# Scan products in 64x32 tiles over two banks each, one bank for gate/up and one for projections, and a new order of work in a tick

## The reference, cut to what matters

```python
# B=2, S=4096, D=512, H=16 heads of Dh=32; mini-batches of MB=16 tokens
k = rope(x @ Wk.T);  v = x @ Wv.T             # per head
W = eye(Dh)                                   # one state per batch and head
for kc, vc in minibatches(k, v):              # 256 steps, one after the other
    z = kc @ W
    W = W - kc.T @ ((z - vc) * (2.0 / (MB * Dh)))
out = (layernorm(zs) * ln_gamma + ln_beta) @ Wo.T
x1 = layernorm(x + out)
h = silu((x1 @ gate_w.T) * gate_s) * ((x1 @ up_w.T) * up_s)      # 1408 wide
y = layernorm(x1 + (h @ down_w.T) * down_s)
```

## Time and profile before

| | |
|---|---|
| median of 3 runs | 2142.03 us (2141.74 to 2142.14) |
| span of the profiled execution | 2140.6 us |
| instructions | 46538 |
| PE busy / PE weight loads busy | 2034.7 us / 1564.8 us |
| DVE / ACT / POOL busy | 1197.3 / 895.1 / 602.6 us |
| mean DMA rate | 82 GB/s |

### The profile page before, as it was taken

The page is one execution under the profiler, slowest core; times in us unless marked ns, Lnnn a source line. Parts: engine busy times, 40 slices in busy tenths (PEclk is TensorE's granted clock), DMA queues, the critical chain, the costliest instruction groups (busy, mean ns, idle before and its releaser), DMA issues.

```text
span 2140.6 us, 46538 instructions
## 1 busy us (share of the span) xinstructions
PE 2034.7 (95%) x16272; PEld 1564.8 (73%) x16272; DVE 1197.3 (56%) x2814; ACT 895.1 (42%) x2258; POOL 602.6 (28%) x651
## 2 busy tenths in 40 slices
PE   7569999999999999999999999999999999999998
PEld 4347777777777777777777777777777777777677
DVE  3575556555556555555655555655555655555553
ACT  2334444444434444434444434444434444444432
POOL 2002323232323232323222323222333322233223
PEclk9779999999999999999999999999999999999999
DMA  7742232212322212232212232212232212232210
GB/s 229 237 133 59 90 87 80 75 52 72 87 89 80 75 52 70 86 89 80 86 39 72 85 91 80 85 48 63 85 90 82 84 50 72 74 90 74 56 35 21
DMA packets 210943, 175.78 MB, mean 82 GB/s; under 512 B 34192, under 2 KB 165520, under 8 KB 210576
## 3 DMA queue, kind: packets, MB, share of 16 engines
q1 hardware_dynamic: 210768, 173.08, 27.0%
HBM read 105.86 MB, written 75.76 MB: 85 GB/s over the span
## 4 chain that ended last, share of the span: by engine, by line
PE 88%; DVE 4%; issue 3%; SPq 3%; ACT 2%; DMA 1%; DVEq 0%; POOL 0%; POOLq 0%; ACTq 0%
PE gu_acc L563 34%; PE work L547 25%; PE down_acc L572 13%; PE z_acc L526 7%; PE state_acc L539 7%; PE work L554 3%; DVE err L722 2%; SPq L290 2%; ACT state L420 2%; DMA z_scr<-v_rows 1%; DVE low_half L733 1%; SPq L275 0%; DMA x_tok<-wkT 0%; DMA z_tok<-z_scr 0%; DMA k_scr<-k_tok 0%
## 5 line engine op out<-in xcount | busy, mean ns | idle before, releaser
L722 DVE TENSOR_TENSOR err<-z_acc,v_rows 32x256 f32<-32x256 f32 x1024 | 430.6, 421 | 736.4 <-PE z_acc L526 700.0
L382 POOL TENSOR_TENSOR hid_lo<-hid,hid_hi 128x256 fp32r<-128x256 f32 x352 | 285.1, 810 | 769.0 <-ACT hid_hi L456 769.0
L420 ACT ACTIVATE state<-state_acc 32x256 f32<-32x256 f32 x1028 | 386.7, 376 | 251.8 <-PE state_acc L539 222.8
L438 ACT ACTIVATE v_rows<-z_acc 128x256 f32<-128x256 f32 x256 | 98.7, 385 | 716.0 <-DVE err L722 716.0
L563 PE MATMUL gu_acc<-x_hi,gw 128*128 128x256 f32 x1408 | 381.8, 305 | 0.5 <-DVE x_lo L780 0.5
L563 PE MATMUL gu_acc<-x_lo,gw 128*128 128x256 f32 x1408 | 346.2, 280 | 0.0
L563 PE MATMUL gu_acc<-x_hi,uw 128*128 128x256 f32 x1408 | 346.0, 279 | 0.0
L563 PE MATMUL gu_acc<-x_lo,uw 128*128 128x256 f32 x1408 | 345.8, 279 | 0.0
L563 PEld LDWEIGHTS gu_acc<-x_hi,gw 128*128 128x128 f32 x1408 | 264.9, 188 | 100.0 <-issue 98.1
L572 PE MATMUL down_acc<-dw,hid_hi 128*128 128x512 f32 x704 | 287.5, 408 | 0.0
L572 PE MATMUL down_acc<-dw,hid_lo 128*128 128x512 f32 x704 | 278.6, 396 | 0.0
(11 more groups left out here) (67 smaller groups left out, 2170.8 us busy)
## 6 DMA issues: line engine op xcount, KB each, us to landing
x_fm<-xT SPq DMA_DIRECT2D x64, 256.0 KB, 4.2
k_scr<-k_tok SPq DMA_DIRECT2D x32, 512.0 KB, 5.1
k_rows<-k_scr SPq DMA_DIRECT2D x512, 32.0 KB, 2.2
v_rows<-v_scr SPq DMA_DIRECT2D x512, 32.0 KB, 1.8
z_scr<-v_rows SPq DMA_DIRECT2D x512, 32.0 KB, 1.6
z_tok<-z_scr SPq DMA_DIRECT2D x32, 512.0 KB, 4.1
x_tok<-x SPq DMA_DIRECT2D x32, 512.0 KB, 3.8
out<-x_tok SPq DMA_DIRECT2D x32, 512.0 KB, 2.8
```

Source lines behind the costliest of these rows:

```text
L382: pool.tensor_tensor(hid_lo[m % RING][:], hid[m % 2][:], hid_hi[m % RING][:].bitcast(F32), ALU.subtract).then_inc(hid_lo_ready, 1)
L420: act.activation(state[q, :, q], state_acc[q, 0:NG * HEAD].rearrange("p (g e) -> p g e", g=NG), ACT.Copy, scale=-STEP).then_inc(state_read ...
L438: act.activation(v_rows[:, i].rearrange("p g c -> p (g c)"), z_acc[:, 0:2 * P], ACT.Copy).then_inc(z_saved, 1)
L722: dve.tensor_tensor(err[q, 2 * j:2 * j + 2, :, :].rearrange("p g h e -> p (g h e)"), z_acc[q, 0:2 * P], v_rows[q, i].rearrange("p g c -> p ...
```

## The change

1. **Scan products.** A 128-row product becomes two 64-row ones in the upper and the lower half of the array (`tile_position=(r*64, j*32)`), so eight tiles of 64x32 work side by side. The block of `state` that a 64-row half needs is 64 wide in place of 128, and the part of `err` that it needs is 128 wide in place of 256. The halves r=0 and r=1 write to two different banks, so `z_acc` and `state_acc` take two banks each. `scan_z` goes from 8 products of 128 columns to 16 of 64, `scan_state` from 4 of 256 to 8 of 128. DVE and ACT read both banks in the same number of instructions, of the same 256 elements for each partition.
2. **Banks.** To free two banks, gate/up has one (`gu_acc`) and the projection scratch has one (`work`). Piece m+1 of gate/up waits until DVE has read piece m (`hid_ready`), and each of batch 1's projections and turns waits until batch 0's result has been read. The turns of x1 go to `gu_acc`.
3. **Order.** Gate/up is in slots 0 to 8, 11 and 13, `down` in 1 to 9, 13 and slot 0 of the next tick; v of batch 1 is projected in quarters in slots 1 to 4, the k turns are in slots 5 and 6, the z turns in 7 and 8, wo in 9 and 10, wk of batch 0 in 12, v of batch 0 in 14 (so a tick earlier than before), wk of batch 1 in 15, the x1 turns in 14 and 15. The scaling of y, its residual and its norm move to slots 1 to 4 of the next tick. DVE, ACT, POOL and the DMA queue follow that order.
4. On PE the values of the scan's waits are computed ahead of the waits (`ahead`).

```diff
--- before.py
+++ after.py
+GU_SLOTS = (0, 1, 2, 3, 4, 5, 6, 7, 8, 11, 13)
+DOWN_SLOTS = (1, 2, 3, 4, 5, 6, 7, 8, 9, 13)
...
-        err = sb("err", [P, NG, HQ, HEAD])
-        state = sb("state", [P, NG, P])
+        err = sb("err", [P, NG // 2, HQ, HEAD])
+        state = sb("state", [P, NG, 2 * HEAD])
...
-        state_acc = bank("state_acc")
-        z_acc = bank("z_acc")
-        gu_acc = [bank("gu_acc0"), bank("gu_acc1")]
+        def bank_pair(name):
+            return ctx.enter_context(nc.psum_tensor(name, [P, 2, 512], F32))
+
+        state_acc = bank_pair("state_acc")
+        z_acc = bank_pair("z_acc")
+        gu_acc = bank("gu_acc")
         down_acc = [bank("down_acc0"), bank("down_acc1")]
-        work = [bank("work0"), bank("work1")]
...
                 if ncc.within():
-                    store_z(ncc, 1, saved[1], z_sent[1])
+                    store_z(ncc, 1, saved[1])
+                if t.within():
+                    if t.past(2):
+                        for half in range(2):
+                            sp.wait_ge(rows_in[half], rows_b)
+                    sp.wait_ge(v_ready, v_first)
+                    sp.dma_start(v_scr[t.par, 0], v_tok[0][:]).then_inc(v_stored, 16)
+                if ncc.within():
+                    sp.wait_ge(z_stored, z_sent[1])
                     if ncc.past(1):
                         sp.wait_ge(zn_turned, c_before)
                     sp.dma_start(z_tok[:], z_scr[:, rows(ncc), :].rearrange("b t f -> t b f")).then_inc(z_tok_in, 16)
+                if t.within():
+                    sp.wait_ge(k_ready, split)
+                    sp.dma_start(k_scr[t.par].rearrange("b t f -> t b f"), k_tok[:]).then_inc(k_stored, 16)
                 if nb.within():
                     if nb.past(1):
                         sp.wait_ge(state_added, scanned)
                     load_rows(nb.par, 1, k_sent[1], v_sent[1])
+                if t.back(-1).within() and t.past(0):
+                    load_x_fm(t.back(-1), split, used)
...
+                if t.within():
+                    sp.wait_ge(v_ready, split)
+                    sp.dma_start(v_scr[t.par, 1], v_tok[1][:]).then_inc(v_stored, 16)
...
+                    if ncc.within() and s == 11:
+                        inverse_root(1, ncc)
+                    if nd.within() and s - 1 in GU_SLOTS:
+                        low_hid(nd, GU_SLOTS.index(s - 1))
+                    if t.within() and s == 1:
+                        add_rotated(t, 1)
+                    if ny.within() and s in (1, 2):
+                        add_residual(ny, s - 1)
+                    if ny.within() and s == 3:
+                        inverse_root(2, ny)
...
+                    if ncc.within() and s in (7, 8):
+                        add_bias(ncc, s - 7)
+                    if nk.within() and s == 13:
+                        add_rotated(nk, 0)
...
-                    act.activation(state[q, :, q], state_acc[q, 0:NG * HEAD].rearrange("p (g e) -> p g e", g=NG),
+                    e = slice(h % 2 * HEAD, (h % 2 + 1) * HEAD)
+                    act.activation(state[q, :, e].rearrange("p (r g) e -> p r g e", r=2),
+                                   state_acc[q, :, 0:P].rearrange("p r (g e) -> p r g e", e=HEAD),
                                    ACT.Copy, scale=-STEP).then_inc(state_ready, 1)
...
+                    if nd.within() and s - 1 in GU_SLOTS:
+                        high_hid(nd, GU_SLOTS.index(s - 1))
+                    if nk.within() and s == 10:
+                        high_x(nk, ncc, 0)
+                    if ncc.within() and s == 8:
+                        high_zn(ncc, t, 1)
+                    if nb.within():
+                        if s % 2 == 0:
+                            save_z(nb, s // 2)
+                        else:
+                            act.wait_ge(state_added, nb.count(4 * NS, 4 * (s // 2) + 4))
+                            copy_state()
+                    if nd.within() and s in GU_SLOTS:
+                        gate(nd, GU_SLOTS.index(s))
+                    if t.within() and s == 4:
+                        copy_v(t, 1)
+                    if ncc.within() and s == 7:
+                        high_zn(ncc, t, 0)
+                    if nk.within() and s == 10:
+                        high_x(nk, ncc, 1)
+                    if nk.within() and s == 14:
+                        copy_v(nk, 0)
+                    if ncc.within() and s in (14, 15):
+                        high_x1(ncc, s - 14)
...
             def scan_z(n, i):
+                loaded, saved, turned = [ahead(v) for v in (n.count(4 * NS, 4 * i + 4), n.count(NS, i), n.count(4, 4))]
+                pe.wait_ge(zeroed, 6)
                 if i == 0:
-                    pe.wait_ge(k_cols_ready, n.count(4, 4))
-                pe.wait_ge(state_ready, n.count(4 * NS, 4 * i + 4))
+                    pe.wait_ge(k_cols_ready, turned)
+                pe.wait_ge(state_ready, loaded)
                 if i >= 1 or n.past(1):
-                    pe.wait_ge(z_saved, n.count(NS, i))
-
-                for g in (*range(0, NG, 2), *range(1, NG, 2)):
-                    j = g // 2
-                    mm = pe.matmul(z_acc[j * HEAD:(j + 1) * HEAD, g % 2 * P:(g % 2 + 1) * P],
-                                   lhsT=k_cols[n.par][:, g, i, :], rhs=state[:, g, :], start=True, stop=True,
-                                   skip_group_check=True, tile_position=(0, j * HEAD))
-                    if g % 2:
-                        mm.then_inc(z_done, 1)
+                    pe.wait_ge(z_saved, saved)
+
+                for odd in range(2):
+                    for r in range(2):
+                        k = slice(r * P // 2, (r + 1) * P // 2)
+                        for j in range(NG // 2):
+                            g = 2 * j + odd
+                            mm = pe.matmul(z_acc[j * HEAD:(j + 1) * HEAD, r, odd * 2 * HEAD:(odd + 1) * 2 * HEAD],
+                                           lhsT=k_cols[n.par][k, g, i, :], rhs=state[k, g, :], start=True, stop=True,
+                                           skip_group_check=True, tile_position=(r * P // 2, j * HEAD))
+                            if odd and r:
+                                mm.then_inc(z_done, 1)
             def scan_state(n, i):
+                loaded, ready = ahead(n.count(32 * NG, 32 * NG)), ahead(n.count(4 * NS, 4 * i + 4))
+                pe.wait_ge(zeroed, 6)
                 if i % (NS // 2) == 0:
-                    pe.wait_ge(rows_in[i // (NS // 2)], n.count(32 * NG, 32 * NG))
-                pe.wait_ge(err_ready, n.count(4 * NS, 4 * i + 4))
-                for h in range(HQ):
-                    q = slice(h * HEAD, (h + 1) * HEAD)
-                    pe.matmul(state_acc[q, 0:NG * HEAD], lhsT=k_rows[:, i, q], rhs=err[:, :, h, :],
-                              start=False, stop=False, skip_group_check=True, tile_position=(0, h * HEAD)
-                              ).then_inc(state_added, 1)
+                    pe.wait_ge(rows_in[i // (NS // 2)], loaded)
+                pe.wait_ge(err_ready, ready)
+                for r in range(2):
+                    k = slice(r * P // 2, (r + 1) * P // 2)
+                    for h in range(HQ):
+                        q = slice(h * HEAD, (h + 1) * HEAD)
+                        mm = pe.matmul(state_acc[q, r, 0:P], lhsT=k_rows[k, i, q], rhs=err[k, :, h, :],
+                                       start=False, stop=False, skip_group_check=True,
+                                       tile_position=(r * P // 2, h * HEAD))
+                        if r:
+                            mm.then_inc(state_added, 1)
...
+            def gate_up(n, m, dt):
+                if m == 0:
+                    pe.wait_ge(x1_lo_ready, n.count(2, 2))
+                else:
+                    pe.wait_ge(hid_ready, n.count(NM, m))
...
+            def turn_z(n, t, b):
+                pe.wait_ge(zn_ready, n.count(2, b + 1))
+                if b == 1:
+                    pe.wait_ge(zn_low, n.count(2, 1))
+                elif t.within():
+                    pe.wait_ge(k_cols_ready, t.count(4, 4))
+                else:
+                    pe.wait_ge(o_added, n.count(2))
+                turn(work, z_tok, b, zn_turned)
+            def project_o(n, b):
+                if b == 0:
+                    if not n.past(1):
+                        pe.wait_ge(w_low, 3 * NC)
+                    pe.wait_ge(zn_low, n.count(2, 2))
+                else:
+                    pe.wait_ge(o_added, n.count(2, 1))
+                project(b, wo, o_done)
+            def turn_x1(n, nd, b):
+                pe.wait_ge(x1_ready, n.count(2, b + 1))
+                if b == 1:
+                    pe.wait_ge(x1_lo_ready, n.count(2, 1))
+                elif nd.within():
+                    pe.wait_ge(hid_ready, nd.count(NM, NM))
+                turn(gu_acc, x1_tok[n.par], b, x1_turned)
...
+                    if t.within() and s == 6:
```

(106 more changed lines are left out.)

349 lines of the change are left out of this document (131 added, 218 removed).

## The result

The changed kernel takes 2092.58 us (median of 4 runs, 2089.24 to 2094.79) against 2141.89 for the kernel before, measured beside it: ratio 0.9769, 95% interval 0.9757 to 0.9781. It is faster by 49 us, where 101 were forecast: 52 are missing; the time lies in the range (2010 to 2105), outside the forecast's own (2018 to 2065).

A forecast was written before the change was run, and what follows sets the result against it. PE was taken to bound the kernel. Per tick -3.4 (scan tiles) - 0.8 (thin slots) + 0.5 (new waits) = -3.7; 29 ticks -107, ticks 2 and 32 -5, end +11: 2041 us, range 2010 to 2105.

The forecast's parts named there:

- the forecast's own: Main case, chance 0.60: 2018 to 2065 us, from 0.2 and 1.5 us of new waits a tick and varying first ticks.
- the slower rival: In `scan_z`, 0.027 us for each load and product pair sets the pace: +3.4 us a tick, 2243 us; chance 0.10.
- the 0.054 for eight: In the scan blocks, a group of 8 instructions with 64 columns each takes 0.054 us, paced by columns.
- The z turn waits: Second z turn on the one scratch bank waits for ACT and DVE to read the first: 0.3 us late each tick.
- the wait for `hid_ready` in slots 0, 5 and 6: Next gate/up piece waits for Silu and scaling: covered, but margin only 0.1 us in slot 0.
- The rival of the order giving back part: Tiles gain, but a low-margin wait is longer, 1.5 to 3 us more a tick: 2085 to 2128 us; chance 0.18.
- The 1.2 at the loop's end stays: At the end of the two-tick loop body, all four engines' standstill of 1.2 us, 0.6 a tick, stays unchanged.
- +8 net: From tick 32 on: tick 32 may gain 3 us, the last ticks' bare waits cost +11.
- the forecast of -2: Stretch up to tick 3: tick 2 may gain 2 us.

The follow-up runs named there:

- unroll_after: The changed kernel with its ticks 4 to 29 written out in place of the hardware loop; 2058.37 us.
- unroll_before: The kernel before with its ticks 4 to 29 written out in place of the hardware loop; 2127.75 us.
- early_turn: The changed kernel with both x1 turns ahead of the projections in slots 14 and 15; 2071.8 us.
- late_turn: The changed kernel with the x1 turn for batch 1 behind all of the last projection of slot 15; 2107.42 us.
- tiles_undone: The changed kernel with the scan products back in 128x32 tiles, one bank each in use, order and other banks as changed; 2164.04 us.
- tail: The changed kernel with a second gate/up bank and separate banks for the two x1 turns in the last ticks only; 2083.08 us.

## Why the prediction was wrong in size

**Right: what bounds, and the scan products.** The chain stayed on PE, the halves run together, and a block went from 0.57 to 0.38, forecast 0.36. The instruction pace that the slower rival feared is 7 ns, which is just the 0.054 for eight that the columns ask for. The first eight starts of a block, into empty tiles, are already 7 ns apart, so by an estimate from them `scan_z` would not gain from more, smaller tiles; that was not tried. The Trainium skill's floor of about 25 ns from start to start ("TensorE: Matmul & The Clock Gate", in the part headed "Wait — 56ns, not 53.3ns?") does not hold for tiles side by side: 32 of them start within some 0.24 us.

**Right: the steady slots.** Slots 1 to 14 came out within 0.1 us of the forecast: 1 to 8 took 3.79 to 4.10 (3.8 to 4.1), 9 4.30 (4.3), 10 and 12 3.38 (3.35), 11 2.46 (2.4), 13 3.40 (3.4), 14 3.82 (3.8). The z turn waits 0.2 (0.3); the wait for `hid_ready` in slots 0, 5 and 6, which I took for the likeliest loss, never shows. The rival of the order giving back part named the right time, 2085 to 2128, but the wrong place: that 2092.6 lies in the stated range is luck, since it was that rival which stretched the range so far. A tick is 59.9 and not 59.5, 12 us in all, from blocks of 0.38 and a slot 15 of 3.9 in place of 3.8.

**Wrong: "The 1.2 at the loop's end stays: nothing in the change shortens the jump."** The jump stayed as long; its cover did not. The standstill went from 1.18 to 1.90 us. The step counted it as a price of the loop, when it is what 3.3 to 4.0 us of branch leave after the PE work already handed over: PE's last product starts 2.4 us after the branch is issued in the kernel before, 1.7 us after it in the changed one. Moving the x1 turn, short and with a wait, into the last slot took that cover away: 12 x 0.72 = 9 us, shown by unroll_after, unroll_before and early_turn; whether by its wait or by its shortness stays open. The same step also left out the clock: 8 x 1.5 = 12 us. That early_turn and unroll_after are free of it shows that it hangs on the standstills; why the changed kernel has 8 falls where kernels with standstills about as long (late_turn 2.01 in the mean, tiles_undone 1.70) have 0 and 2 stays open.

**Mis-sized: the ends.** In the end I had +8 net and it was +22: a piece waits 0.42, not 0.3, and the stretches at half clock weigh there as well (from tick 32 on the kernel before has 15 us of them in its trace, the changed one 30). tail gave back 12.5 of it; the rest was not split up. At the start the forecast of -2 was +7: I did not follow ticks 0 to 2 through the single scratch bank, where seven waits of 0.8 to 1.7 us stand between 20 and 44 us with nothing to fill them. Also, PE stands for 1.8 us ahead of tick 3, where before there was no gap. This is not the loop's branch: the branch that opens tick 3 takes 0.09 us in both kernels. PE waits there for a value that says whether the weights have a low part, and the chain shows it come late, behind x1's low part on DVE:

```profile
158.04 0.69 DVE x_lo L850
158.73 0.08 DVE low_half L876
...
158.94 0.39 POOL low_most L422
159.33 1.26 issue
160.59 0.58 PE z_acc L577 x29
```

In the kernel before DVE is through with it at 150.2, 3.1 us ahead of tick 3, while PE is at work. No run changed this. The four places make up the difference: 12 us in the steady ticks, some 20 at the loop's end, 14 at the end and 9 at the start, 55 for the 52 missing. The other 3 are the forecast's own: it took 0.6 of standstill in each of 29 ticks for the kernel before, 17 us, where 12 x 1.18 is 14.

## What to carry to other kernels

At a hardware loop's back edge look for the last semaphore wait on the bounding engine, and count the work queued behind it: it covers the branch. Put long products there, not short ones, and count on no more than some ten of them, the most that stood there in these traces. A reordering of slots is judged at the loop's edge, the first and the last ticks as well as in the steady tick, since waits that other stages hide in the middle stand bare there. When small products are already paced by columns in column tiles, splitting the contraction over row halves and two banks halves the time of the columns (here 0.19 of the 0.21 us forecast for each block), as long as the instruction pace (7 ns here) allows it.

## What the runs showed of the hardware

- The loop's branch takes PE's sequencer 3.3 to 4.0 us. Over 12 jumps the loop's end cost 16 us in a kernel whose last product starts 2.4 us after the branch is issued, and 35 in one where it starts after 1.7, the stretches at half clock included. The Trainium skill ("Advanced Engine Details and Errata", section "Control Flow Timing") has about 108 ns for a compare-and-branch; the traces here show some thirty times that for this jump back over a long body, and 0.04 to 0.09 us for the other engines' branches in the same place and for PE's where no jump is taken. Each long branch of PE has a 16 KB DMA of instructions inside it. That this load is what takes the time was not tried.
- The sequencer runs ahead of PE: when the loop's branch is issued, 9 or 10 weight loads of this tick are still to start, in every kernel with the loop. A wait that is satisfied while PE has such work adds nothing to the standstill even when it stands last (late_turn, 2.01 us against 1.90).
- Standstills of 0.9 to 1.5 us at the jump never brought the granted clock down (12 in early_turn, 12 in the kernel before). Those of 1.5 to 2.4 us did in 0, 2, 7 or 8 cases of 12, depending on the kernel, each time for 3.4 us, which cost about 1.5 us.
- Products in eight tiles of 64x32 start one in 7 ns, 32 of them with their weight loads in 0.24 us.
